# State-space stage: GpSimd multiplies by C in four instructions of one state each, and TensorE's sums wait state by state

## The reference, cut to what matters

```python
hidden, gate = split(x @ in_proj_w)                 # 1024 channels each
u  = silu(causal_conv4(hidden) + conv_b)
dt, B, C = split(u @ x_proj_w)                      # 128, 16, 16, each normalised
dt = softplus(dt @ dt_proj_w + dt_proj_b)
s[t, ch, n] = exp(dt[t, ch] * A[ch, n]) * s[t-1, ch, n] + dt[t, ch] * u[t, ch] * B[t, n]
y[t, ch]    = sum over n of s[t, ch, n] * C[t, n]   # 16 states n
out = ((y + u * D) * silu(gate)) @ out_proj_w
```

## Time and profile before

| | |
|---|---|
| median of 3 runs (lowest, highest) | 5323.17 us (5321.68, 5325.96) |
| the profiled execution | 5325.68 us, of which the span of its instructions 5323.8 us |
| TensorE busy | 4817.2 us, 90% of the span |
| VectorE busy | 4447.0 us, 84% |
| GpSimd busy | 3155.8 us, 59% |
| ScalarE busy | 2689.8 us, 51% |
| products by C on GpSimd (L336) | 1024, mean 2359 ns |
| scans (L649) | 2048, mean 1260 ns |
| TensorE's granted clock | mean 0.969 of full speed |

### The profile page before, as it was taken

How to read it: one execution, slowest core, us unless ns; L and a number is a source line. 1 busy time by engine, 2 the same in 40 slices (tenths; PEclk the granted TensorE clock), 3 DMA queues, 4 the chain that set the end, 5 groups by cost and what they waited for, 6 DMA issues and landing times. The chain is left out here.

```text
span 5323.8 us, 108656 instructions
## 1 busy us (share of the span) xinstructions
PE 4817.2 (90%) x44199; PEld 2788.8 (52%) x44199; DVE 4447.0 (84%) x7289; ACT 2689.8 (51%) x4364; POOL 3155.8 (59%) x1639
## 2 busy tenths in 40 slices
PE   6899999999999999999999999987499999999973
PEld 3344444444444444444444444433388888888862
DVE  3989889898998989889898898985578888888876
ACT  3666666666666666666566665652133333333320
POOL 1676776767767676676766767675144443444436
PEclk9999999999999999999999999998699999999995
DMA  2222212222222222222222222221300000000003
GB/s 86 84 92 85 97 72 104 94 82 104 73 104 89 88 102 75 97 89 87 101 82 96 86 90 102 75 96 64 129 26 28 26 28 26 28 28 26 28 22 78
DMA packets 117198, 394.68 MB, mean 74 GB/s; under 512 B 26720, under 2 KB 28384, under 8 KB 83808
## 3 DMA queue, kind: packets, MB, share of 16 engines
q1 hardware_dynamic: 107040, 383.95, 20.5%
q0 software_dynamic: 6336, 0.18, 0.3%
q10 hardware_dynamic: 3328, 3.61, 0.2%
HBM read 348.20 MB, written 39.50 MB: 73 GB/s over the span
## 5 line engine op out<-in xcount | busy, mean ns | idle before, releaser
L336 POOL TENSOR_TENSOR s<-s,Cb 128x1024 f32<-128x1024 f32 x1024 | 2394.1, 2359 | 996.2 <-DVE state L654 991.9
L649 DVE TENSOR_TENSOR_SCAN s<-s,state,BU 128x512 f32<-128x512 f32 x2048 | 2453.2, 1260 | 368.2 <-PE BU L738 347.7
L505 ACT ACTIVATE s<-dt,ch 128x512 f32<-128x512 f32 x2048 | 1307.0, 715 | 718.9 <-PE Y L755 717.4
L755 PE MATMUL Y<-s,ident 64*64 64x512 f32 x8192 | 1010.4, 609 | 67.0 <-POOL s L336 66.7
L681 PE MATMUL PJ<-xnT,w_in 128*128 128x512 f32 x2048 | 947.0, 606 | 30.1 <-ACT xnT L372 15.3
L738 PEld LDWEIGHTS BU<-spread,dtuT 32*128 32x128 f32 x16384 | 512.3, 189 | 529.7 <-DVE s L649 338.3
L738 PE MATMUL BU<-spread,dtuT 32*128 32x128 f32 x16384 | 609.9, 286 | 146.4 <-DVE s L649 145.7
L681 PEld LDWEIGHTS PJ<-xnT,w_in 128*128 128x128 f32 x2048 | 369.9, 190 | 502.7 <-issue 423.8
L755 PEld LDWEIGHTS Y<-s,ident 64*64 64x64 f32 x8192 | 277.6, 134 | 563.6 <-issue 527.7
L729 PE MATMUL PJ<-w_out,u 128*128 128x512 f32 x1024 | 471.3, 604 | 7.9 <-ACT xnT L372 6.4
L1105 POOL TENSOR_TENSOR x1t<-x1t,bias_b 128x512 f32<-128x512 f32 x64 | 83.0, 1296 | 398.9 <-DVE xa L1291 398.9
(11 more groups left out here) (223 smaller groups left out, 6951.4 us busy)
## 6 DMA issues: line engine op xcount, KB each, us to landing
Cb<-bc SPq DMA_DIRECT2D x256, 1024.0 KB, 4.8
res<-in_x SPq DMA_DIRECT2D x64, 256.0 KB, 5.0
x<-res SPq DMA_DIRECT2D x64, 256.0 KB, 5.1
x1t<-x SPq DMA_DIRECT2D x64, 256.0 KB, 2.6
out<-r_t SPq DMA_DIRECT2D x64, 256.0 KB, 2.0
xt<-in_x SPq DMA_DIRECT2D x31, 512.0 KB, 5.7
rows_of<-out SPq DMA_DIRECT2D x10, 512.0 KB, 7.5
out<-rows_of SPq DMA_DIRECT2D x10, 512.0 KB, 3.6
```

The lines of the kernel that those rows point to most:

```text
L336: nc.gpsimd.tensor_tensor(pair, pair, Cb[q % 2][:, 2 * part * T:2 * part * T + 2 * T], ALU.mult).then_inc(z_ready, 1)
L505: nc.scalar.activation(s[k % SLOTS][:, n, :], dt[p % 2][:, gi, :], ACT.Exp, scale=ch[:, 2 * p + gi, 7 + 4 * nq + n:8 + 4 * nq + n]).then_i ...
L649: nc.vector.tensor_tensor_scan(s[k % SLOTS][:, n, :], s[k % SLOTS][:, n, :], BU[:, n::4], state[:, b, k, n:n + 1], ALU.mult, ALU.add).then ...
L755: last_ = nc.tensor.matmul(Y[r][y_rows(r, gi), :], ident[rows, rows], s[(k_even + gi) % SLOTS][rows, n, :], start=False, stop=(n == 3 and ...
```

## The change

GpSimd's product with C goes from two instructions of two states to four of one state, each with its own increment of `z_ready`, so the semaphore counts 4 a unit where it counted 2. Inside `y_sum` TensorE waits ahead of each state's 4 matmuls for just that state of the odd unit (the even unit's products are before it in GpSimd's queue), where it waited once ahead of 8 for both. SyncE's wait ahead of the C load is counted anew, for the same point.

```diff
--- before.py
+++ after.py
@@ -257,7 +257,7 @@
                             load_res(i_prev, b_prev, c_prev, 0)
                             load_res(i_prev, b_prev, c_prev, 1)
                     if k % 2 == 0:
-                        held(z_ready, c * 2 * U + 2 * k)
+                        held(z_ready, 4 * (c * U + k))
                         if k // 2 + 1 < U // 2:
                             load_c(k // 2 + 1, b)
                         elif not last:
@@ -331,10 +331,9 @@
                     if k % 2 == 0:
                         wait(pool, c_loaded[q % 2], 16 * (c * (U // 4) + (q % (U // 2)) // 2 + 1))
                     wait(pool, state_saved, c * U + k + 1)
-                    for part in range(2):
-                        pair = s[k % SLOTS][:, 2 * part:2 * part + 2, :].rearrange("p n t -> p (n t)")
-                        nc.gpsimd.tensor_tensor(pair, pair, Cb[q % 2][:, 2 * part * T:2 * part * T + 2 * T],
-                                                ALU.mult).then_inc(z_ready, 1)
+                    for n in range(4):
+                        one = s[k % SLOTS][:, n, :]
+                        nc.gpsimd.tensor_tensor(one, one, Cb[q % 2][:, n * T:(n + 1) * T], ALU.mult).then_inc(z_ready, 1)
                     if k == 0 and not first:
                         wait(pool, dbu_ready, c * U)
                         spread_b(c, 3)
@@ -747,8 +746,10 @@
                         nc.tensor.matmul(Y[r][y_rows(r, gi), :], skip_w[rows, 2 * p + gi, :], u[slot][rows, 2 * p + gi, :],
                                          start=True, stop=False, tile_position=(64 * r, y_rows(r, gi).start))
 
-            def y_sum(k_even, part):
+            def y_sum(k_even, part, units_done):
                 for n in range(2 * part, 2 * part + 2):
+                    pe.wait_ge(z_ready, units_done + n + 1)
+                    pe.sem_inc(pe_steps, 1)
                     for r in range(2):
                         rows = slice(64 * r, 64 * r + 64)
                         for gi in range(2):
@@ -789,9 +790,7 @@
                         wait(pe, y_ready, c * G + 2 * (k_even // UP))
                         pe.sem_inc(pe_steps, 1)
                         skip_product(k_even // UP, b)
-                    pe.wait_ge(z_ready, c * 2 * U + 2 * k - 1 if part == 0 else c * 2 * U + 2 * (k - 1))
-                    pe.sem_inc(pe_steps, 1)
-                    y_sum(k_even, part)
+                    y_sum(k_even, part, 4 * (c * U + k - 1 if part == 0 else c * U + k - 2))
 
                 def passed():
                     pe.drain().then_inc(steady.full, 1)
@@ -865,8 +864,7 @@
 
             periods(pe, body)
             for part in range(2):
-                pe.wait_ge(z_ready, NCH * 2 * U - 1 + part)
-                y_sum(U - 2, part)
+                y_sum(U - 2, part, 4 * (NCH * U - 1))
             pe.wait_ge(y_ready, G * NCH)
             for j in range(NT):
                 if j >= 2:
```

## The result

| | kernel before | changed kernel |
|---|---|---|
| median of the runs on one chip, us | 5322.43 (5321.67 to 5325.96, 4 runs) | 5353.77 (5352.99 to 5354.03, 4 runs) |
| profiled execution, us | 5325.68 | 5354.03 |
| TensorE waits for GpSimd's products | 66.7 us, 70 waits | 15.7 us, 27 waits |
| one period of the state-space stage, us | 223.67 | 225.45 |

The changed kernel takes 1.0054 times as long, with 1.004 to 1.0068 as the interval: slower by 0.54%, 31 us in the medians and 28.4 us between the two profiled executions. The forecast was 5350.

A forecast was written before the change was run, and what follows sets the result against it. TensorE and VectorE were taken as near the bound, GpSimd with 66 us to spare a period. Profiled 5325.68 + 29 (held VectorE pieces) - 2 (last period) = 5352.7, the median 2.5 lower: 5350 us; 8-in-10 range 5328 to 5380.

The forecast's parts named there:

- TensorE's waits for GpSimd, 0: Units 12, 18, 22 and 28: earlier sums gain 0, since ScalarE's xT copy or VectorE's scans hold TensorE next.
- Rival (b): TensorE's four waits for GpSimd a period are on the path: 60 waits x 0.75 = 45 us less, 5278; chance 0.05.
- The last period, -2: Last period: unit 14's sum and the last sums each start 1.1 us earlier, together -2 us.
- The waits in the sums, 0: 512 added waits, each with an increment, in TensorE's sums: a satisfied wait was taken to cost 0.
- Rival (d): Waits inside a sum cost up to 0.14 us: up to 47 us more, 5397, or 5368 without the shift; chance 0.07.
- D = 0.32: D is how much later a unit's GpSimd products end: four take 5.00 us instead of 4.68, so 0.32 us.
- Rival (a): D is at most 0.05, GpSimd's time going by elements alone; slack swallows it: 5321 to 5325; chance 0.11.
- (c): D is 0.62, from increments or VectorE between products: 4.3 us a period, 64 us, 5385; chance 0.07.
- VectorE's pieces stand until GpSimd's instruction ends, 7 D - 0.3 a period: Units 15, 16, 18, 19, 21, 22 each add D, unit 20 D - 0.3: 1.94 us a period, +29 in 15.
- +29 - 2 = 27: Whole forecast shift: +29 us from VectorE's held pieces in 15 periods, -2 us from the last period's earlier sums.

## Why the forecast came out, step by step

**TensorE's waits for GpSimd, 0.** Right in all four. Unit 12 was forecast to win 0.75 and lose it at ScalarE's xT; it won 0.55 and lost it there, the wait growing from 0.96 to 1.50. Unit 18 has 0.94 in place of 0.22 for VectorE. In unit 28 the sum starts 0.80 us sooner behind the unit's B product and takes 0.38 longer, and the next B product is where it was. Rival (b), 45 us faster, is out: the 51 us of waits for GpSimd that went bought no time in these periods.

**The last period, -2.** Mis-sized: it came to nothing. The two head starts are there. From unit 14's B product to unit 15's it takes 7.82 us instead of 9.07, and the last sums start 1.40 us behind the last products' start instead of 2.39 and take 6.06 instead of 6.28. But between them the gain is lost. The changed kernel is 28.65 us late up to unit 14, 26.1 by unit 18, and 29.8 at the last reduction. TensorE's granted clock falls again and again in this period, at other places in the two traces: of the 18 B products from unit 14 on, 11 take more than 1.3 us after the change and 7 before (1.17 at full clock). Behind the last sums it is 28.6 us late. The forecast took the two gains by themselves and left out what stands between them. (213.07 for 213.82 us from unit 24 to unit 24 is only a part of this.) How much of the loss is the change's doing and how much differs from one execution to the next, one trace of each does not show.

**The waits in the sums, 0.** Nearly. Skip product to sum takes 0.90 us as before, and a sum whose products are done takes 1.95 to 1.99. Where the wait is not yet satisfied, as in units 12 and 28, the sum takes 2.17 and 2.33: over 2 us at full clock, which had been named as a sign of being wrong, but it is a wait for data and not the cost of a satisfied wait. The waits alone cost 0.17 us a period with pairs and nothing with the shortened products, and I had no term for it. Rival (d), 0.14 in each of 337 units, is out by a factor of 12 or more: 47 us forecast for it, some 2.6 (15 x 0.17) in the periods and 3.9 between the medians measured.

**D = 0.32.** The four products take 4.96 us (median of the trace), not 5.00; two pairs take 4.67, so D is 0.285. This is the term that was mis-sized, by 0.035 us. Rival (a) wanted 0.05 or less, (c) 0.62. Most of the 0.035 lies in the duration, 1.272 us (median) for the 1.28 that came from another stage's rows; the overlap of two consecutive products is 0.043 for the 0.04 assumed.

**VectorE's pieces stand until GpSimd's instruction ends, 7 D - 0.3 a period.** Where and how much came out: six units with a step of D, a small one in unit 20, none in 14 and 17, none left over from 27. With the measured D it is 7 x 0.285 - 0.3 = 1.70, against 1.77 measured; the forecast said 1.94. The other 0.1 or so arises in units 4 to 6 (the B product of unit 6 is 0.13 late), where the normalisation is held in the same way; I had not looked there. The shorter last product that took D away took the loss away, the kernel with half the split cost 0.69, and units 14 to 21 bring nearly all of it: the step is shown, not only argued.
The sentence itself was too coarse. "Until GpSimd's instruction ends" holds for the product that runs when VectorE asks; a further product behind it waits for VectorE or runs beside it. And "with both inputs in SBUF, and this copy" left out an instruction with one tile as input, the normalisation of unit 4. In the changed kernel VectorE asks during the last product, as the prediction said, so the sum is the same. The Trainium skill (SBUF — State Buffer, "Who interferes with whom") has it as a lock that one instruction holds to its end, and both runs with a small last product agree with that reading (copy's end at 2240.28 under a product until 2240.54). The copy that stood until the memset's end, too, shows that more than one instruction can pass before VectorE is let in.

**The sum.** Followed through the two traces, the changed kernel is 0.85 us late at the stage's first B product (in the versions that keep GpSimd's two products that start lies between 114.2 and 116.1 us, so this is no effect of the change), 2.0 more by unit 24 of the first period, and 25.8 more over the next 14 (1.84 on average, since some periods lose more than the typical 1.77). That makes 27.8 for the 15 periods. The last period adds nothing and what follows the stage takes 0.2 off: the span is 28.4 longer. The forecast had +29 - 2 = 27 in its own time. Its errors have opposite signs: a D too large by 0.035 makes 3.7 us too much (15 x 7 x 0.035), the units 4 to 6 left out some 2 too little, and the 2 of the last period, which did not come, again 2 too little. That the number came out so close is in part luck; where the loss arises and how large a step is are not. The medians lie 31.3 us apart, 3 more than the two profiled executions, within what these medians can tell; the forecast had taken 2.5 us off for the median, and the changed kernel's median is 0.3 under its profiled execution.

**What the forecast did not see.** It priced the two halves of the change apart, and they are not independent. Four products without the state-by-state waits are 0.8% slower than before rather than 0.5%. Of these further 13 us some 8 come from unit 28, which then stands idle for 1.65 us and in five of 15 periods runs its sum at half clock; the rest lies in 0.2 us a period and in the last period. The waits that I gave 0 keep the clock up there.

## What to carry to other kernels

An engine with 66 us to spare in 224 can still be on the path: look for instructions of another engine that stretch until an instruction of the idle one ends, with no semaphore between them, and price what you add to it by the places where that happens, counting slack once. A wait of TensorE that shrinks is worth what the next wait behind it allows, and here ScalarE and VectorE stood right behind. If GpSimd's work has to be split, what counts is which of its products is running when VectorE asks, so the last piece should be short, or VectorE should ask at a border: with the last product in two, the loss fell from 0.54% to 0.27%.

## What was new about the chip

- A split of one GpSimd product of 128x1024 f32 into two of 128x512 costs 0.142 us where nothing stands between them (4.67 us for two pairs, 4.96 for four).
- A VectorE copy that already waits gets in between two GpSimd products. A small product of 0.33 us behind the pair did not hold it; a memset of 0.27 us did (0.43 us for the copy, ended 0.02 behind the memset). Both kernels put the small instruction in the same place and behind the same kind of wait, so the difference lies in the instruction itself, its operation or its shape; which of the two I have not separated.
- A VectorE TENSOR_SCALAR with a single tile of 128x512 f32 as input is held too: it ends 0.28 us behind GpSimd's product and takes up to 0.72 us instead of 0.53.
- The lock works in both directions. In the changed kernel with the early reduction, a product of GpSimd that starts under a VectorE product with two SBUF inputs takes 1.71 us instead of 1.27:
```profile
2260.55 1.71 POOL L336 TENSOR_TENSOR s<-s,Cb 128x512 f32<-128x512 f32 x1 [3.19 <-DVE state L619]
```
- With 1.65 us of idle time ahead of the sum of unit 28, TensorE's granted clock fell from 2.4 to 1.2 GHz for 3.4 us in five of 15 periods, and not in the other ten. With 1.33 to 1.50 us (the kernel before) or 0.41 us in the same place it never fell.
